# Attention's divided rows turned by SyncE's transposing DMAs as two 16-bit parts, and an output projection on those parts

## The chip, the cores and the metric

The kernel runs on one core of a Trainium2 chip. A core has TensorE (PE; its weight loads are shown as PEld), VectorE (DVE), ScalarE (ACT), GpSimd (POOL) and SyncE (SP), which issues most DMAs. The metric is device time in microseconds (us) of one launch; lower is better.

## The reference

One pre-norm transformer block: attention with a residual, then a mixture of experts with a residual, over 16 sequences of 512 tokens and 256 channels, all float32.

```python
x = L0_attn_x                                    # (16, 512, 256)
x = x + attn(layernorm(x))
x = x + moe(layernorm(x))

def attn(x):                                     # 16 heads of 16 channels
    q, k, v = split(x @ W_attn + b_attn)
    q, k = rope(q), rope(k)                      # angles by head, not by position
    att = softmax(causal(q @ k.T / sqrt(16)))
    y = att @ v                                  # put together to (16, 512, 256)
    return y @ W_proj + b_proj                   # the part that the change is about
```

The mixture (8 experts, the best 2 for each token, and a shared one) is not touched.

## The kernel before

The attention part goes over 16 batches of 512 tokens (`NB`), each in 4 groups of 4 heads (`NG`) and 5 units per group (`UN`): 20 slots per batch, written **g.s** here (slot 2.3 is unit 3 of group 2). Each engine has a `body` that is written out by slot. Tables of slots near the top (`O_T`, `DIVIDE`, `PROJ`, `QK_LOAD` ...) say in which slot an engine does a step; where it stands within the slot is set by the order of the lines of `body`. Engines run their own instructions in order and wait for each other by semaphores.

In every slot TensorE computes a unit's scores into the one pair of banks `pair_s` (`scores`, L1633 and L1653), VectorE takes row maxima from them (`row_max`, L1151 to L1157), and the next slot's scores wait for these. A group's maxima are turned (L1666), made into 16-bit "shift rows" by ScalarE (L885), and brought into row 48 of the tile `q_op` by SyncE (`load_shift`, L448, slot g.2, two DMAs). From the slot g.3 that follows, TensorE computes the scores a second time, transposed and with the shift (`shifted`, L1680; the first one waits for the shift rows), ScalarE takes exponentials (L876), GpSimd cuts off what lies above the diagonal (`select`, L683), and TensorE mixes the values (`mix`, L1706, piece 0 in a slot g.0). `mix`'s output goes to `o_t` (ScalarE, L917).

Beside this, q, k and v of the next batch are made: projections on TensorE (L1571), `qk_rows` on ScalarE, a split in a 16-bit high and low part on GpSimd (`qk_high` L657, `qk_low` L662), stores to DRAM by SyncE (`store_qk`, L426, in slots 2.3 and 0.2) and twelve loads for each half of the heads into `q_op` and `k_op` (`load_qk`, L440, two in each of six slots from the store's slot on; the first waits until the stores have landed).

The batch before is finished meanwhile, in four quarters of 128 tokens (q = 0 to 3) and two halves (j): `o_t` is turned to rows (`transpose_o`, L1722, slots `O_T`), divided by the sums of the softmax (`divide`, L1166 and L1169, slots `DIVIDE`) into `y`, turned again by float32 transposes on TensorE (`transpose_y`, L1730, slots 2.3 and 0.3), copied from PSUM to `y_t` by ScalarE (L934), multiplied with `wp` in float32 (`project_out`, L1741: half 0 in slots 3.3 and 3.4, half 1 whole in slot 1.1), and added to the input and the bias (`residual`, L1180). Then come a layer norm, a split in 16-bit parts and stores to DRAM.

A float32 `matmul` line leaves two records in the trace. After batch 15 two more bodies finish the last batches (the drain). SyncE then reads the stored rows back with transposing DMAs of 512 KB (`logit_columns`, L537), from which TensorE makes the router's logits; behind these the shared expert and the routed experts follow until the end.

The products of 16-bit parts have one helper, which leaves out the product of the two low parts:

```python
for (lh, ll), (rh, rl) in pairs:
    for a, m in ((lh, rh), (lh, rl), (ll, rh)):
        last = nc.tensor.matmul(out, a, m, start=(i == 0), stop=(i == n - 1))
```

## Time and profile before

| | us |
|---|---|
| median of 3 runs | 1665.31 |
| lowest and highest | 1664.85, 1670.92 |
| profiled execution, first to last instruction | 1663.0 |
| batch 8, from its first scores (406.35) to the next batch's (450.23) | 43.88 |
| first scores of batch 0 and of batch 15 | 47.1, 714.9 |
| first matmul of the shared expert | 817.3 |

A row of the time line tells when an instruction began, how long it took, its engine, its line and its tiles (out <- in); in brackets, how long the engine was idle before it and who ended that. The chain of waits goes back from the last instruction of a stretch: at each step to what released it, or to the instruction before it on its engine.

### The profile page before, as it was taken

The page shows a single profiled execution, that of the slowest core. Times are in us where ns is not written, and L with a number is a line of the kernel's source. Part 1 is how long each engine was busy: PE and PEld are TensorE (multiplying, and loading weights), DVE is VectorE, ACT ScalarE, POOL GpSimd, SP SyncE. Part 2 cuts the span into 40 slices and gives each one's busy share as a digit, 9 for nine tenths or more (in the row PEclk, how much of TensorE's full clock was granted, in tenths as well). Part 3 has the DMA queues.
Part 4 walks back from the last instruction along what each step waited for, and adds up shares of the span by engine and source line. Part 5 has one row for each costly group of instructions (what it writes and reads, how often), then busy time and mean ns, then how long its engine had stood idle before and what let it go on. Part 6 is the DMA issues. An engine that isn't in the chain of part 4 may idle for free.

```text
span 1663.0 us, 42374 instructions
## 1 busy us (share of the span) xinstructions
PE 1530.9 (92%) x14774; PEld 1112.8 (67%) x14777; DVE 1053.8 (63%) x1856; ACT 837.1 (50%) x1257; POOL 898.9 (54%) x1123
## 2 busy tenths in 40 slices
PE   3689999999999999977888889999999999999996
PEld 2345555555555555533777778888888888888885
DVE  7568888888888888867377877753333333333332
ACT  1266666666666666655232235534444444444442
POOL 2145555555555555544114667737666666666652
PEclk9699999999999999988699999999999999999999
DMA  2333333333333333353956744346655566556652
GB/s 82 96 90 90 116 116 107 105 112 107 105 113 105 101 110 113 96 124 77 197 162 179 196 113 101 96 110 106 99 103 100 98 102 104 97 99 104 99 81 36
DMA packets 283849, 180.76 MB, mean 109 GB/s; under 512 B 161201, under 2 KB 274353, under 8 KB 283698
## 3 DMA queue, kind: packets, MB, share of 16 engines
q1 hardware_dynamic: 244914, 130.39, 30.4%
q0 software_dynamic: 30208, 35.81, 14.1%
q10 hardware_dynamic: 8576, 12.58, 2.3%
q8 instruction: 91, 1.49, 0.4%
q14 instruction: 60, 0.49, 0.1%
HBM read 84.04 MB, written 60.30 MB: 87 GB/s over the span
## 4 chain that ended last, share of the span: by engine, by line
PE 69%; DVE 10%; DMA 7%; SPq 5%; issue 3%; ACT 3%; POOL 3%; DVEq 0%; POOLq 0%; ACTq 0%
PE bank L1571 20%; PE pair_s L1845 14%; PE bank L1706 7%; PE bank L1845 7%; PE pair_t L1845 7%; PE pair_s L1633 4%; SPq L440 3%; PE pair_t L1680 3%; PE bank L1741 3%; DMA qk_d<-qkl 2%; ACT prob L876 2%; DVE early L1494 1%; PE pair_s L1653 1%; POOL prob L683 1%; PE bank L1722 1%
## 5 line engine op out<-in xcount | busy, mean ns | idle before, releaser
L876 ACT ACTIVATE prob<-pair_t 128x1024 f32<-128x1024 f32 x320 | 327.7, 1024 | 231.0 <-PE pair_t L1680 226.1
L683 POOL TENSOR_SCALAR_AFFINE_SELECT prob<-prob 128x256 f32<-128x256 f32 (+1 forms) x448 | 199.3, 459 | 332.2 <-ACT prob L876 327.7
L803 POOL DMA_INDIRECT out_x<-ysb,tok_rows x136 | 218.8, 1609 | 166.2 <-ACT ysb L1011 115.5
L985 ACT CAST early<-early 128x512 f16<-128x512 f32 (+1 forms) x208 | 125.3, 602 | 336.7 <-DVE early L1494 336.7
L1500 DVE TENSOR_TENSOR early<-early 128x512 f16<-128x512 f32 (+1 forms) x208 | 139.8, 672 | 141.5 <-ACT early L985 141.5
L1494 DVE SCALAR_TENSOR_TENSOR early<-pair_s,h_s,sg 128x512 f32<-128x512 f32 (+1 forms) x104 | 75.9, 730 | 236.9 <-PE pair_s L1845 233.7
L1571 PE MATMUL bank<-wbuf,early 128*128 x1632 | 190.3, 273 | 5.2 <-issue 3.8
L1845 PE MATMUL pair_s<-xt,wbuf 128*128 128x256 f16 (+1 forms) x1728 | 193.9, 267 | 0.1
L765 POOL DMA_INDIRECT tok_d<-tok_w,dest_i x128 | 136.6, 1067 | 104.2 <-DVE dest_i L1420 52.8
L1706 PE MATMUL bank<-prob,v_op 128*32 128x512 f32 (+3 forms) x2048 | 181.0, 448 | 5.2 <-POOL prob L683 5.2
L1151 DVE TENSOR_REDUCE mx<-pair_s 128x2 f32<-128x1024 f32 x128 | 156.8, 1225 | 44.3 <-PE pair_s L1653 42.7
L1845 PEld LDWEIGHTS pair_s<-xt,wbuf 128*128 x1728 | 163.4, 98 | 19.8 <-issue 0.2
L1571 PEld LDWEIGHTS bank<-wbuf,early 128*128 128x128 f16 x1632 | 158.8, 98 | 25.3 <-issue 6.6
L784 POOL DMA_INDIRECT xrow<-xhl_d,tok_rows x136 | 136.3, 1002 | 55.0 <-issue 37.5
L1633 PE MATMUL pair_s<-k_op,q_op 48*128 48x512 f16 (+3 forms) x1024 | 128.7, 310 | 33.9 <-DVE mx L1151 11.5
L1633 PEld LDWEIGHTS pair_s<-k_op,q_op 48*128 48x128 f16 x1024 | 34.8, 94 | 153.7 <-DVE mx L1151 68.7
L1154 DVE TENSOR_REDUCE mx<-pair_s 128x2 f32<-128x768 f32 x128 | 122.0, 953 | 18.9 <-PE pair_s L1653 17.5
L1680 PE MATMUL pair_t<-q_op,k_op 49*128 49x512 f16 (+3 forms) x1024 | 124.7, 301 | 9.9 <-DMA q_op<-m_row 7.8
L977 ACT ACTIVATE sg<-pair_s,silu_s 128x512 f32<-128x512 f32 (+1 forms) x104 | 69.6, 670 | 81.9 <-PE pair_s L1845 68.2
L1845 PE MATMUL bank<-xt,wbuf 128*128 128x256 f16 (+1 forms) x864 | 103.1, 267 | 0.0
L1845 PE MATMUL pair_t<-xt,wbuf 128*128 128x256 f16 (+1 forms) x864 | 102.8, 267 | 0.0
L1845 PE MATMUL pair_s<-xrow,wsh 128*128 128x256 f16 x720 | 86.1, 274 | 16.4 <-DVE early L1494 16.3
(274 smaller groups left out, 2751.0 us busy)
## 6 DMA issues: line engine op xcount, KB each, us to landing
q_op<-qk_d SPq DMA_DIRECT2D x192, 64.0 KB, 2.6
k_op<-qk_d SPq DMA_DIRECT2D x192, 64.0 KB, 2.7
x_in<-in_L_attn_x SPq DMA_DIRECT2D x16, 512.0 KB, 4.1
qk_d<-qkh SPq DMA_DIRECT2D x32, 256.0 KB, 2.2
qk_d<-qkl SPq DMA_DIRECT2D x32, 256.0 KB, 2.6
xres<-in_L_attn_x SPq DMA_DIRECT2D x16, 512.0 KB, 4.7
x_d<-x SPq DMA_DIRECT2D x32, 256.0 KB, 2.2
xhl_d<-xhl SPq DMA_DIRECT2D x32, 256.0 KB, 2.6
```

Of the source, the lines that this page charges most:

```text
L683: last = nc.gpsimd.affine_select(out=v, in_=v, compare_op=ALU.is_ge, fill=0.0, base=0, pattern=[[0, v.shape[1]], [1, P]], channel_multipli ...
L765: pool.indirect_dma_start(out=tok_d, out_offset=bass.IndirectOffsetOnAxis(ap=dest_i[:, t, k:k + 1], axis=0), in_=tok_w[:, t, k, :], in_off ...
L784: pool.indirect_dma_start(out=xrow[:, k % GATHERED], out_offset=None, in_=xhl_d, in_offset=bass.IndirectOffsetOnAxis(ap=tok_rows[:, k, 0:1 ...
L803: pool.indirect_dma_start(out=out, out_offset=bass.IndirectOffsetOnAxis(ap=tok_rows[:, k, 0:1], axis=0), in_=ysb[:, k % ROWS_AHEAD], in_of ...
L876: nc.scalar.activation(prob[:, half, u].rearrange("p a n -> p (a n)"), pair_t[:].rearrange("p a n -> p (a n)"), ACT.Exp, scale=exp_by).the ...
L1151: last = nc.vector.tensor_reduce(dst[:, :, u, 3], pair_s[:], AX_X, ALU.max)
L1500: nc.vector.tensor_tensor(htl2[:, par, 2 * hh:2 * hh + 2, 0:w], hb2[:, hh, 0:2 * w].rearrange("p (c n) -> p c n", c=2), hth2[:, par, 2 * h ...
L1571: last = nc.tensor.matmul(out, a, m, start=(i == 0), stop=(i == n - 1))
L1633: nc.tensor.matmul(ps_s[a][:, lo:lo + P * (q + 1)], q_op[64 * a:64 * a + KR, par, pair, P * q:P * (q + 1)], k_op[64 * a:64 * a + KR, par, ...
L1680: last = nc.tensor.matmul(ps_t[a][:, lo:lo + n], k_op[rows, par, pair, P * k:P * (k + 1)], q_op[rows, par, pair, P * k:], start=start, sto ...
L1706: last = nc.tensor.matmul(ps_o[32 * h:32 * h + 32, P * k:], v_op[:, vpar, k, GH * gg + h, :], pr[:, unit, h % 2, lo:lo + n], start=(piece ...
L1845: last = nc.tensor.matmul(out[:, w * k:w * k + w], stationary, rows[:, x, 0:w], start=(i == 0), stop=(i == 3 * CC - 1))
```

## The change

The tile `y` is now divided and scaled by a power of two in one step. GpSimd splits each quarter into a 16-bit high and low part (`y_split`: a cast and a subtraction into `y_hl`). When a half has both quarters, SyncE turns the 128x1024 16-bit row block by one transposing DMA into `y_t` (`y_columns`). The transposes of `y` on TensorE and ScalarE's copy are gone. `project_out` multiplies 16-bit parts: per 128 tokens six 16-bit matmuls in place of two float32 ones. The scale is taken out in `residual`. Scales and parts of the weights (`wp_h`, `wp_l`, in the tile `cs` that is free by then) are made once, in the prologue; the weights arrive in the tile `y`. The quarters' transposes and divisions move: quarter 2 from slot 3.2 to 3.0, quarter 3 from slots 0.1 and 0.2 to 3.2.

```diff
-        O_T = ((1, 4), (2, 2), (3, 2), (0, 1))
-        DIVIDE = ((2, 1), (2, 2), (3, 2), (0, 2))
-        Y_T, Y_OUT = ((2, 3), (0, 3)), ((3, 1), (0, 4))
+        O_T = ((1, 4), (2, 2), (3, 0), (3, 2))
+        DIVIDE = ((2, 1), (2, 2), (3, 0), (3, 2))
+        Y_SPLIT, Y_COLUMNS = ((2, 2), (2, 3), (3, 1), (3, 3)), ((3, 0), (0, 0))
...
+            def y_columns(bp, j):
+
+                sp.wait_ge(S["yl_done"], 4 * bp + 2 * j + 2)
+                sp.sem_inc(S["sp_passed"], 1)
+                if some(2 * bp + j):
+                    sp.wait_ge(S["pr_in"], 2 * bp + j)
+                    sp.sem_inc(S["sp_passed"], 1)
+                sp.dma_start_transpose(y_t[:], y_hl[:, j].rearrange("p t n -> p (t n)")).then_inc(y_turned[j], 16)
...
                             sp.dma_start(xres[:], xv[b - 1]).then_inc(S["res_in"], 16)
+                        for j, bp in heads_here((g, s), Y_COLUMNS, b, prev, prev2):
+                            y_columns(bp, j)
...
+            def y_split(bp, q):
+
+                k, j = 4 * bp + q, q // 2
+                pool.wait_ge(S["y_done"], k + 1)
+                if q % 2 == 0 and some(bp):
+                    pool.wait_ge(y_turned[j], 16 * bp)
+                high = y_hl[:, j, q % 2, 0:C]
+                nc.gpsimd.tensor_copy(high, y[:, q % 2]).then_inc(S["yh_done"], 1)
+                pool.wait_ge(S["yh_done"], k + 1)
+                nc.gpsimd.tensor_tensor(y_hl[:, j, q % 2, C:], y[:, q % 2], high, ALU.subtract
+                                        ).then_inc(S["yl_done"], 1)
...
-                        for j, bp in heads_here((g, s), Y_OUT, b, prev, prev2):
-                            k = 2 * bp + j
-                            act.wait_ge(S["yT_in"], k + 1)
...
-                            nc.scalar.copy(y_t[:].rearrange("p t c n -> p (t c n)"),
-                                           ps_y[:]).then_inc(S["yT_done"], 1)
...
-                nc.vector.tensor_tensor(y[:, q % 2].rearrange("p (h d) -> p h d", d=HD), ov[:, :, 0:HD],
-                                        rec[:, q % 2].unsqueeze(2).broadcast_to([P, H, HD]),
-                                        ALU.mult).then_inc(S["y_done"], 1)
+                if some(k - 1):
+                    dve.wait_ge(S["yl_done"], k - 1)
...
+                nc.vector.scalar_tensor_tensor(out=y[:, q % 2].rearrange("p (h d) -> p h d", d=HD),
+                                               in0=ov[:, :, 0:HD], scalar=vp_scale[:, 0:1],
+                                               in1=rec[:, q % 2].unsqueeze(2).broadcast_to([P, H, HD]),
+                                               op0=ALU.mult, op1=ALU.mult).then_inc(S["y_done"], 1)
...
-            def transpose_y(bp, j):
-                pe.wait_ge(S["y_done"], 4 * bp + 2 * j + 2)
-                for t in range(2):
-                    for c in range(2):
-                        last = nc.tensor.transpose(ps_y[:, P * (2 * t + c):P * (2 * t + c + 1)],
-                                                   y[:, t, P * c:P * (c + 1)], ident[:])
...
                 if t == 0:
-                    pe.wait_ge(S["yT_done"], 2 * bp + j + 1)
+                    pe.wait_ge(y_turned[j], 16 * bp + 16)
...
-                for c in range(2):
-                    last = nc.tensor.matmul(ps_m[:, 256 * t:256 * t + 256], y_t[:, t, c, :], wp[:, c, :],
-                                            start=(c == 0), stop=(c == 1))
+                last = products(ps_m[:, 256 * t:256 * t + 256],
+                                [((y_t[:, 4 * t + c, :], y_t[:, 4 * t + CC + c, :]), (wp_h[:, c, :], wp_l[:, c, :]))
+                                 for c in range(CC)])
```

Where this puts instructions, first SyncE from the stores of slot 2.3 to the shift rows of slot 3.2 in a middle batch, before (`qk_d` is q and k in DRAM, `m_row` the shift rows; a "waits" names semaphores):

```order
L426 DMA qk_d<-qkl 128x2x512
L440 DMA q_op<-qk_d 16x4x512 [waits qks0,t_in]
L440 DMA k_op<-qk_d 16x4x512
L440 DMA q_op<-qk_d 16x4x512
L440 DMA k_op<-qk_d 16x4x512
L440 DMA q_op<-qk_d 16x4x512
L440 DMA k_op<-qk_d 16x4x512
L440 DMA q_op<-qk_d 16x4x512
L440 DMA k_op<-qk_d 16x4x512
L448 DMA q_op<-m_row 1x8x128 [waits m_done]
```

and the same place now:

```order
L434 DMA qk_d<-qkl 128x2x512
L448 DMA q_op<-qk_d 16x4x512 [waits qks0,t_in]
L448 DMA k_op<-qk_d 16x4x512
L448 DMA q_op<-qk_d 16x4x512
L448 DMA k_op<-qk_d 16x4x512
L448 DMA q_op<-qk_d 16x4x512
L448 DMA k_op<-qk_d 16x4x512
L498 DMA_TRANSPOSE y_t<-y_hl 128x8x128 [waits yl_done,pr_in]
L448 DMA q_op<-qk_d 16x4x512
L448 DMA k_op<-qk_d 16x4x512
L456 DMA q_op<-m_row 1x8x128 [waits m_done]
```

The new DMA stands behind six of the eight loads and ahead of two loads and the shift rows, with two waits of its own.

GpSimd in slots 3.3 to 0.0, before (`prob` is the select's tile, `qkl` the low parts of the next batch's q and k):

```order
L657 CAST qkh<-qkf 128x512 [waits qks1,qkf_done]
L683 AFFINE_SELECT prob<-prob 128x4x128 [waits exp_done]
L683 AFFINE_SELECT prob<-prob 128x2x128 [waits exp_done]
L662 TENSOR_TENSOR qkl<-qkf,qkh 128x512 [waits qkh_done]
L683 AFFINE_SELECT prob<-prob 128x2x128 [waits exp_done] x2
```

and now:

```order
L683 TENSOR_TENSOR y_hl<-y,y_hl 128x256 [waits yh_done]
L717 AFFINE_SELECT prob<-prob 128x4x128 [waits exp_done]
L717 AFFINE_SELECT prob<-prob 128x2x128 [waits exp_done]
L696 TENSOR_TENSOR qkl<-qkf,qkh 128x512 [waits qkh_done]
L681 CAST y_hl<-y 128x256 [waits y_done]
L683 TENSOR_TENSOR y_hl<-y,y_hl 128x256 [waits yh_done]
L717 AFFINE_SELECT prob<-prob 128x2x128 [waits exp_done] x2
L717 AFFINE_SELECT prob<-prob 128x2x128
```

The fourth quarter's split stands between `qk_low` of slot 3.3 and the select of slot 3.4.

TensorE in slot 1.1, from its scores to those of slot 1.2, before (`bank` is a rotating PSUM bank):

```order
L1633 MATMUL pair_s<-k_op,q_op 128x512 [waits max_done]
L1633 MATMUL pair_s<-k_op,q_op 128x512
L1653 MATMUL pair_s<-mask,pick 128x64 x4
L1680 MATMUL pair_t<-q_op,k_op 128x384 [waits exp_done]
L1680 MATMUL pair_t<-q_op,k_op 128x384
L1680 MATMUL pair_t<-q_op,k_op 128x128 x2
L1741 MATMUL bank<-wp,y_t 128x256 [waits m_done,yT_done]
L1741 MATMUL bank<-wp,y_t 128x256 x3
L1633 MATMUL pair_s<-k_op,q_op 128x384 [waits max_done]
```

and now:

```order
L1689 MATMUL pair_s<-k_op,q_op 128x512 [waits max_done]
L1689 MATMUL pair_s<-k_op,q_op 128x512
L1709 MATMUL pair_s<-mask,pick 128x64 x4
L1736 MATMUL pair_t<-q_op,k_op 128x384 [waits exp_done]
L1736 MATMUL pair_t<-q_op,k_op 128x384
L1736 MATMUL pair_t<-q_op,k_op 128x128 x2
L1627 MATMUL bank<-cs,y_t 128x256 [waits m_done,y_cols1]
L1627 MATMUL bank<-cs,y_t 128x256 x11
L1689 MATMUL pair_s<-k_op,q_op 128x384 [waits max_done]
```

The four float32 matmuls (eight records) have become twelve 16-bit ones in the same place, which wait for the DMA's landing in place of ScalarE's copy.

## Rows read from the trace of the kernel before

**Rows 1.** The page, the whole span: busy time, its share and the instructions of each engine.

```profile
PE 1530.9 (92%) x14774; PEld 1112.8 (67%) x14777; DVE 1053.8 (63%) x1856; ACT 837.1 (50%) x1257; POOL 898.9 (54%) x1123
```

**Rows 2.** Stretches: us, busy PE, PEld, DVE, ACT, POOL, clock, DMA share, GB/s.

```profile
406.35:450.23 43.88, 42.72 (x437) 23.30 (x438) 37.92 (x73) 30.20 (x43) 24.37 (x43) 1.00 0.34 104
733.57:743.81 10.24, 8.01 (x53) 2.64 (x53) 3.20 (x4) 4.26 (x6) 3.06 (x6) 0.50 0.67 128
```

**Rows 3.** Time line, TensorE, scores of slot 2.4 (columns as explained above).

```profile
437.21 0.39 PE L1633 MATMUL pair_s<-k_op,q_op 48*128 48x256 f16 x4 [0.20 <-DVE mx L1155]
```

**Rows 4.** Chain of waits, slots 2.2 to 3.3 of batch 8: start, us, what.

```profile
435.48 1.14 POOL qkl L662
...
437.17 2.74 DMA qk_d<-qkl
...
440.07 0.32 SPq L440
...
443.24 0.43 SPq L440
...
443.79 0.64 SPq L448
...
444.47 1.83 DMA q_op<-m_row
...
446.35 0.39 PE pair_t L1680 x2
...
447.31 1.06 PE bank L1741 x4
```

**Rows 5.** Time line, ScalarE, GpSimd and TensorE, slots 3.2 to 0.0 of that batch.

```profile
441.66 0.25 ACT L885 ACTIVATE m_row<-bank 16x128 f16<-16x128 f32 x1
...
448.57 1.15 POOL L662 TENSOR_TENSOR qkl<-qkf,qkh 128x512 f16<-128x512 f32 x1
...
450.26 0.42 POOL L683 TENSOR_SCALAR_AFFINE_SELECT prob<-prob 128x256 f32<-128x256 f32 x1 [0.54 <-ACT prob L876]
...
451.16 1.06 PE L1706 MATMUL bank<-prob,v_op 128*32 128x512 f32 x8
```

**Rows 6.** Line 1680: why TensorE sat idle before it: releaser, us, times.

```profile
  DMA q_op<-m_row: 17.5, 17
```

**Rows 7.** Issues of transposing DMAs, 128 KB (L580), 256 KB (L550): ns least/median/most.

```profile
L580 SPq DMA_TRANSPOSE xt<-xrow x136: 1190/1260/2399, 1092.4 to 1634.8; - x136
...
L550 SPq DMA_TRANSPOSE xrow<-xhl_d x30: 1234/1242/2152, 821.2 to 1067.9; - x30
```

**Rows 8.** Chain of waits, slot 1.1: TensorE's projection of half 1.

```profile
419.32 1.97 PE bank L1741 x8
```

**Rows 9.** Time line, VectorE: the residual behind that projection.

```profile
421.32 0.69 DVE L1180 TENSOR_TENSOR x<-bank,xres 128x512 f32<-128x512 f32 x1 [1.08 <-PE bank L1741]
```

**Rows 10.** Chain of waits in the routed experts: matmuls of 128x256 on 16-bit parts.

```profile
984.12 2.62 PE bank L1571 x24
```

**Rows 11.** Groups by line, GpSimd: count, busy us, mean ns, idle before and releaser.

```profile
L662 POOL TENSOR_TENSOR qkl<-qkf,qkh 128x512 f16<-128x512 f32 x60 | 69.6, 1161 | 0.1
...
L657 POOL CAST qkh<-qkf 128x512 f16<-128x512 f32 x60 | 36.6, 610 | 20.4 <-ACT qkf L846 20.4
```

**Rows 12.** Time line in the drain: SyncE's first 512 KB transpose, TensorE's last logits.

```profile
799.26 2.32 SPq L537 DMA_TRANSPOSE qkl<-xhl_d  x1
...
816.67 0.80 PE L1571 MATMUL bank<-gate_hl,qkl 128*128 128x8 f16 x24 [1.30 <-DMA qkl<-xhl_d]
```

**Rows 13.** Chain of waits, batch 15, SyncE's issues around a 512 KB transpose.

```profile
725.18 2.04 SPq L537
...
728.82 1.59 SPq L440
...
731.48 0.68 SPq L448
```

**Rows 14.** Time line, TensorE, first shifted matmul of batch 15's slot 0.3.

```profile
733.96 0.61 PE L1680 MATMUL pair_t<-q_op,k_op 49*128 49x512 f16 x2 [2.44 <-DMA q_op<-m_row]
```

More of the change, by code:

```diff
@@ L139, in build @@
         wal = sb_a("wal", [P, 2, 3 * C], F32R)
-        wp = sb_a("wp", [P, 2, C], F32)
+        wp_h, wp_l = (cs[:, k].bitcast(F16).rearrange("p (c n) -> p c n", c=2) for k in range(2))
         bcol = sb_a("bcol", [P, 4], F32)
@@ L168, in build @@
         y = sb_a("y", [P, 2, C], F32)
-        y_t = sb_a("y_t", [P, 2, 2, P], F32)
+        y_hl = sb_a("y_hl", [P, 2, 2, 2 * C], F16)
+        y_t = sb_a("y_t", [P, 2 * 2 * CC, P], F16)
+        wp = y
         xres = sb_a("xres", [P, NT, C], F32)
@@ L715, in body @@
                                 input_rstd(b + 2)
+                        for q, bp in heads_here((g, s), Y_SPLIT, b, prev, prev2):
+                            y_split(bp, q)
                         for j, bp in halves_here((g, s), RSTD_B, b, prev, prev2):
@@ L1138, in prologue_qkv, with output_scales @@
                     first_low(i)
+            def output_scales():
+                dve.wait_ge(S["vp_topped"], 1)
+                link.link(dve, nc.vector.tensor_scalar(vp_top[:], vp_top[:], 1e-30, None, ALU.max))
+                link.link(dve, nc.vector.tensor_scalar(vp_top[:].bitcast(I32), vp_top[:].bitcast(I32),
+                                                       0x7F800000, None, ALU.bitwise_and))
+                link.link(dve, nc.vector.reciprocal(vp_inv[:], vp_top[:]))
+                nc.vector.tensor_scalar(vp_scale[:, 0:1], vp_inv[:, 0:1], 16.0, None, ALU.mult)
+                nc.vector.scalar_tensor_tensor(out=out_scale[:], in0=vp_top[:, 0:1], scalar=2.0 ** -18,
+                                               in1=vp_top[:, 1:2], op0=ALU.mult, op1=ALU.mult)
+                nc.vector.tensor_scalar(vp_scale[:, 1:2], vp_inv[:, 1:2], 2.0 ** 14, None, ALU.mult
+                                        ).then_inc(S["vp_done"], 1)
+                dve.wait_ge(S["wph_done"], 1)
+                nc.vector.scalar_tensor_tensor(out=wp_l, in0=wp[:], scalar=vp_scale[:, 1:2], in1=wp_h,
+                                               op0=ALU.mult, op1=ALU.subtract).then_inc(S["wpl_done"], 1)
             prologue()
             prologue_qkv()
+            output_scales()
             def row_max(G, g, u):
@@ L1179, in residual @@
                     dve.wait_ge(x1_stored[j], 16 * bp)
-                nc.vector.tensor_tensor(x1[:, j].rearrange("p t c -> p (t c)"), ps_m[:],
-                                        xres[:, 2 * j:2 * j + 2].rearrange("p t c -> p (t c)"), ALU.add
-                                        ).then_inc(S["x1_done"], 1)
+                nc.vector.scalar_tensor_tensor(out=x1[:, j].rearrange("p t c -> p (t c)"), in0=ps_m[:],
+                                               scalar=out_scale[:],
+                                               in1=xres[:, 2 * j:2 * j + 2].rearrange("p t c -> p (t c)"),
+                                               op0=ALU.mult, op1=ALU.add).then_inc(S["x1_done"], 1)
             def residual_stats(bp, j):
```

34 lines of the change are left out of this document (20 added, 14 removed).

## The prediction

> **What bounds the kernel now.** I read the page first: TensorE is busy for 92% of the span [rows 1]. A busy share does not say what the removal of TensorE work is worth, so I next asked for a table of stretches. One whole batch of the attention part takes 43.88 us with TensorE busy for 42.72, VectorE for 37.92 and GpSimd for 24.37 [rows 2]. TensorE looks like the bound, with VectorE 6 us behind. But the twenty slots of a batch do not add up freely: `scores` of a slot waits for all row maxima of the slot before it, since there is one pair of banks for scores. In slot 2.4, for example, TensorE starts 0.20 us late, released by VectorE's maximum [rows 3]. A slot whose TensorE work is already shorter than scores plus maximum gains nothing by losing more.
>
> So I read the chain of waits over a batch. From slot 2.2 to slot 3.3 it is not TensorE's at all [rows 4]: GpSimd's `qk_low` (435.48, 1.14 us), SyncE's two stores of q and k to DRAM, whose landing takes 2.74 us from 437.17, eight load issues on SyncE from 440.07 to 443.67 (0.43 us each and a gap of 0.04), then the issue of the shift rows at 443.79, its landing 1.83 us after the second of its two issues, and the first shifted matmul at 446.35. The shift rows had been ready since 441.91 [rows 5]: SyncE's queue kept them 1.9 us, and the matmul starts the moment they land. This is not one batch's bad luck. TensorE's first shifted matmul is ended by these rows 17 times, for 17.5 us together [rows 6]. In the other batches the order on SyncE is the same, so I take the slack of this chain as zero to 0.3 us.
>
> **The change, part by part.** Sums are made against the profiled execution, 1663.0 us from first to last instruction; the median of the runs, 1665.3, is 2.3 above it, and I add that at the end. N is 14: batches 1 to 14 have both a previous batch to project and a next one to load.
>
> *SyncE's transposing DMA of half 0 (slot 3.0).* It stands in SyncE's queue behind six of the eight load issues and ahead of the last two and of the shift rows, which are thus held up by all of it. Its data are old by then (GpSimd's second split ends a slot earlier, and SyncE comes to it six issues of 0.47 after 440.07, at 442.9), so its waits cost only their passing: two more gaps and counts, about 0.16 us by the gaps of rows 4. The issue itself: this trace has no DMA of 128 x 1024 between two SBUF tiles. Two rows bracket it [rows 7]: SBUF to SBUF with half the bytes holds SyncE for 1.26 us (least 1.19), and DRAM to SBUF with the same bytes for 1.24. Doubling the bytes between those two added nothing, so I take 1.26; the upper end is twice that, 2.5, if a source in SBUF pays by bytes; the lower end is an ordinary issue, 0.43. Taken: 1.26 + 0.16 = 1.42 us per batch, all of it on the path, N x 1.42 = **+19.9** (ends 8.3 and 37).
> The Trainium skill, page Advanced Engine Details and Errata, section X-Bar Transpose (TRN2), says that transposing DMAs are as fast as regular ones. As to the time for which they hold the queue, the rows disagree: 1.26 against 0.43. By that rule the term would be 14 x (0.43 + 0.16) = 8.3 us.
>
> *What this chain covers.* Between slots 2.2 and 3.3 TensorE now has time to spare, so work moved or removed there is worth nothing: the transposes of `y` that leave slot 2.3, the transposes of `o` that move from slot 3.2 to 3.0 and from 0.1 to 3.2 (0.6 us more in 3.0), the first three splits on GpSimd, and VectorE's divisions in their wider form. Without that cover the added transposes in 3.0 would cost up to 0.6 us a batch. The transposes that leave slot 0.3 free TensorE where it waits for the maximum anyway: zero. ScalarE's copy of `y_t` was off the path: zero.
>
> *The projection of half 1, slot 1.1.* Here the chain runs along TensorE: eight float32 records take 1.97 us [rows 8], and VectorE's residual waits for them, idle 1.08 us [rows 9]. They become twelve 16-bit matmuls of 128x256. Twenty-four such matmuls take 2.62 us elsewhere [rows 10], 0.109 each, so twelve take 1.31: -0.66. VectorE, which carries this stretch right behind TensorE, may return a little with its wider residual; I take -0.56. N x -0.56 = **-7.8** (ends -9.2 and -4).
>
> *The projection of half 0, slot 3.3.* Four records of 1.06 us [rows 4] become six matmuls, 0.65: -0.41. But the fourth split stands on GpSimd right behind `qk_low` of this slot, which ends at 449.72, and ahead of the next select (450.26) that `mix` of slot 0.0 needs at 451.16 [rows 5]. A cast of 128x512 takes 0.61 us and a subtraction 1.16 [rows 11]; half as wide and with two gaps, a split is about 1.0. The select then ends near 451.25 and `mix` starts near 451.3, where with the gain it would have been ready at 450.75. The gain is lost, and 0.14 more. N x 0.14 = **+2.0** (ends -5.7, if splits are cheaper, and +7).
>
> *Half 1's transposing DMA, slot 0.0.* SyncE waits there for the fourth split and may hold up the shift rows of slot 0.2. At slot 0.3 no first shifted matmul of the trace is ended by these rows, so I take zero; if that room is gone, the price is that of half 0.
>
> *The drain.* After the last batch SyncE issues transposing DMAs of 512 KB one behind the other (from 799.26 on, 2.32 us the first) and TensorE's last logits wait for the last of them [rows 12]. Two `y` transposes now stand among these, 1.4 each: +2.8; the second also waits until half 0 is projected. Taken **+3** (ends 1 and 7).
>
> *Prologue.* Maxima and splits of the weights run while VectorE waits for GpSimd and TensorE for the first keys; zero, at most 3 us once.
>
> Sum: 19.9 - 7.8 + 2.0 + 3 = +17.1, so 1680.1 for the profiled execution and **1682** for the median.
>
> **The rivals.** *A: the transposing DMA costs SyncE more than its issue.* The trace has a precedent: in the last batch a transposing DMA of 512 KB (2.04 us) went out among the loads at 725.18, one load issue after it took 1.59 in place of 0.43, and the shift rows followed only at 731.48 [rows 13]. TensorE then stood idle for 2.44 us [rows 14], and its granted clock fell to 0.50, the 1.2 GHz level, for 10.24 us [rows 2]. Half the bytes could add 0.6 us of such stalling per batch (+8), an issue of 2.5 adds 17, and a fallen clock in a few batches 2 to 4 us each (+8). That gives about 1700 to 1715. Against it: the stall I expect is mostly 1 to 1.5 us, shorter than the one before that fall.
>
> *B: the queue is held for no longer than by an ordinary DMA.* Then the first term is 8.3 and the sum 5.5: 1671, no change that can be measured. The skill's rule quoted above would end here; the rows on the time of issue speak against it. A split cheaper than I think, together with an issue at its least, ends here too.
>
> *C: faster.* The shift rows are not held up: the transposing DMA's issue falls into time in which SyncE would have waited. Then only the projections count: -7.8 - 5.7 + 3 = -10.5, or 1655. It decides at a delay of about 0.2 us per batch in place of 1.42. For it: TensorE is the busiest engine and loses work in four slots of each batch. Against it: SyncE issues the eight loads without a break and the shift rows right behind them [rows 4], so there is no waiting time for the DMA to fall into.
>
> **How the numbers follow.** Within 0.5% is about what a measurement of this kernel can tell from no change: 1657 to 1673.6. My forecast, 1674 to 1692, has 0.48; A, up to about 1715, has 0.20; B, 1658 to 1673, has 0.20; C has 0.12. Hence faster 0.12, same 0.20, slower 0.68. The range leaves out C's lower half and A's upper end: 1656 to 1708.
>
> **What would show it.** In the profile after, a transposing DMA on SyncE between the sixth and the seventh load issue, 1.2 to 1.3 us long; the issue of the shift rows 3.3 us after they are ready in place of 1.9; TensorE's first shifted matmul of slot 3.3 idle for 1 to 1.5 us in nearly every batch, where the whole kernel had 17.5 us before; batches of about 45 us in place of 44. Slot 1.1 should be shorter by 0.6 us, `mix` of slot 0.0 should wait for GpSimd's select, and the shared experts should start about 3 us later relative to the last batch. The prediction is wrong if the shift rows go out as soon as before, if the new issue takes 0.5 us or over 2, or if the granted clock falls in slot 3.3.

## The result, and the profile after

The changed kernel takes 1686.97 us (median of 4 runs, 1683.8 to 1687.95), the kernel before 1665.08 beside it: a ratio of 1.0125, interval 1.0105 to 1.0146. It is slower by 1.25%, as forecast; the forecast was 1682, the range 1656 to 1708. The profiled execution spans 1684.8 us, 21.8 more than before.

The page's line of busy times, which answers [rows 1]:

```profile
PE 1501.2 (89%) x14774; PEld 1089.4 (65%) x14777; DVE 1068.9 (63%) x1865; ACT 820.7 (49%) x1226; POOL 957.6 (57%) x1252
```

TensorE is busy for 30 us less and the kernel is 22 us longer. The work did leave TensorE; what was lost is waiting. The rows that answer [rows 4] are the chain of waits in the same place, slots 2.2 to 3.3 of batch 8 (start, us, what):

```profile
445.87 1.17 POOL qkl L696
...
447.60 2.52 DMA qk_d<-qkl
...
450.27 0.32 SPq L448
...
452.51 0.43 SPq L448
...
453.12 1.27 SPq L498
...
454.44 0.58 SPq L448
...
455.61 0.68 SPq L456
...
456.33 1.70 DMA q_op<-m_row
...
458.07 0.41 PE pair_t L1736 x2
```

Six load issues run to 452.94; the transposing DMA (L498) stands there from 453.12 for 1.27 us; the load behind it takes 0.58 us in place of 0.43; the shift rows follow at 455.61. ScalarE had them ready at 452.39, so SyncE's queue kept them 3.2 us, where it had been 1.9 [rows 5]. TensorE's time line in the same batch (start, us, engine, line, operation, tiles; in brackets idle time and its end):

```profile
451.79 0.66 PE L1773 MATMUL bank<-ident,o_t 128*128 128x128 f32 x4
...
458.07 0.39 PE L1736 MATMUL pair_t<-q_op,k_op 49*128 49x512 f16 x2 [0.74 <-DMA q_op<-m_row]
...
458.97 0.83 PE L1627 MATMUL bank<-cs,y_t 128*128 128x256 f16 x6
```

The transposes of quarter 2 now stand in slot 3.0 (0.66 us); the first shifted matmul of slot 3.3 waits 0.74 us for the shift rows although TensorE has more to do on its way there. Over the whole kernel, from the view of waits (engine and line, what it waited for: us in total, times, longest), the kernel before and the changed one:

```profile
PE pair_t L1680 <- DMA q_op<-m_row: 7.8, 7, 2.4
```

```profile
PE pair_t L1736 <- DMA q_op<-m_row: 17.4, 16, 1.9
```

TensorE's first shifted matmul waits for the shift rows 16 times in place of 7, for 17.4 us in place of 7.8. (In [rows 6] the waits of TensorE's weight loads, 10 of 9.7 us, are counted with those of the matmuls; the prediction reads them as 17 waits of one kind.)

To compare runs I cut each of batches 1 to 14 into three stretches, by the starts that the time line gives, and sum each over the 14 batches. **A** goes from the first scores of slot 0.0 to those of slot 2.2, **B** from there to the first shifted matmul of slot 3.3 (SyncE's chain), **C** from that to the next batch's first scores. In us, with the runs of the experiments below:

| kernel | A | B | C | median | ratio to before |
|---|---|---|---|---|---|
| before | 374.1 | 190.9 | 54.2 | 1665.1 | |
| after | 374.2 | 211.7 | 52.9 | 1687.0 | 1.0125 |
| e1_gap | 371.4 | 218.7 | 52.6 | 1696.7 | 1.0202 |
| e2_price | 372.9 | 216.2 | 64.9 | 1703.6 | 1.0244 |
| e3_plain | 376.3 | 202.8 | 50.0 | 1677.5 | 1.0087 |
| e4_late_split | 366.2 | 211.9 | 50.8 | 1679.3 | 1.0094 |
| e5_gaps | 376.2 | 221.4 | 61.0 | 1708.2 | 1.0256 |
| e6_gap_early | 374.8 | 205.3 | 50.0 | 1680.2 | 1.0100 |
| e7_gap_late | 369.4 | 204.9 | 50.0 | 1676.7 | 1.0069 |
| e8_placed | 395.5 | 205.0 | 50.0 | 1699.3 | 1.0210 |
| e9_idle_price | 372.5 | 190.3 | 54.2 | 1663.3 | 0.9991 |
| e10_gap_price | 373.2 | 196.6 | 55.6 | 1670.9 | 1.0033 |
| e11_best_split | 367.5 | 197.4 | 51.6 | 1668.3 | 1.0032 |
| e12_cover | 374.9 | 212.8 | 57.6 | 1694.4 | 1.0180 |

Ratios are against runs of the kernel before beside each (medians 1662.4 to 1665.1); the intervals are given below where they matter, and are 0.13% to 0.33% wide to each side. Two medians of this table that were taken beside different runs of the kernel before can thus differ by up to 2.7 us without a cause in the kernels. The stretches are those of one profiled execution each.

### The profile page after: what moved, and what is told of

It is laid out like the page before. It is cut to its first block, busy times and chain, and to the rows that moved or that the text cites. A ratio compares the mean times of both kernels' runs of the same rounds, so it can differ in the third digit from the quotient of the medians.

```text
span 1684.8 us, 42580 instructions
## 1 busy us (share of the span) xinstructions
PE 1501.2 (89%) x14774; PEld 1089.4 (65%) x14777; DVE 1068.9 (63%) x1865; ACT 820.7 (49%) x1226; POOL 957.6 (57%) x1252
## 3 DMA queue, kind: packets, MB, share of 16 engines
q0 software_dynamic: 30208, 35.81, 13.8%
q8 instruction: 91, 1.49, 0.4%
## 4 chain that ended last, share of the span: by engine, by line
PE 56%; DMA 11%; SPq 10%; DVE 9%; POOL 5%; issue 4%; ACT 4%; ACTq 0%; DVEq 0%; POOLq 0%
PE bank L1627 19%; PE pair_s L1888 13%; PE bank L1888 7%; PE pair_t L1888 7%; SPq L448 6%; PE bank L1762 4%; DMA qk_d<-qkl 4%; ACT prob L914 3%; PE pair_s L1689 3%; POOL qkl L696 2%; DMA k_op<-qk_d 2%; PE pair_t L1736 2%; POOL prob L717 2%; DMA q_op<-m_row 2%; DVE early L1550 1%
## 5 line engine op out<-in xcount | busy, mean ns | idle before, releaser
L717 POOL TENSOR_SCALAR_AFFINE_SELECT prob<-prob 128x256 f32<-128x256 f32 (+1 forms) x448 | 195.5, 450 | 277.0 <-ACT prob L914 261.6
L1627 PEld LDWEIGHTS bank<-wbuf,early 128*128 128x128 f16 x1632 | 158.7, 98 | 24.7 <-issue 6.0
L1736 PE MATMUL pair_t<-q_op,k_op 49*128 49x512 f16 (+3 forms) x1024 | 123.9, 299 | 20.9 <-DMA q_op<-m_row 17.4
```

The source lines that it names most:

```text
L717: last = nc.gpsimd.affine_select(out=v, in_=v, compare_op=ALU.is_ge, fill=0.0, base=0, pattern=[[0, v.shape[1]], [1, P]], channel_multipli ...
L1736: last = nc.tensor.matmul(ps_t[a][:, lo:lo + n], k_op[rows, par, pair, P * k:P * (k + 1)], q_op[rows, par, pair, P * k:], start=start, sto ...
```

## The experiments

The theory: the cost is the time for which the transposing DMA holds SyncE's queue ahead of the shift rows, on a chain without slack. Its rivals: the DMA's traffic slows the loads and the shift rows wherever it stands; or the moved and added work on TensorE and GpSimd costs it.

### e2_price and e9_idle_price: the same DMA, twice, in the kernel before

Only this is added to the kernel before (`turned` is a spare tile, `wah` a part of the weights); in e2_price at slot 3.0 behind the loads, in e9_idle_price at slot 0.2 behind the shift rows:

```diff
+                        if prev and (g, s) == (3, 0):
+                            if some(b - 1):
+                                sp.wait_ge(S["turned_in"], 16 * (b - 1))
+                                sp.sem_inc(S["sp_passed"], 1)
+                            sp.dma_start_transpose(turned[:], wah[:, 0, 0:512].bitcast(F16)
+                                                   ).then_inc(S["turned_in"], 16)
```

> The kernel before, with one addition: in slot 3.0 of each batch SyncE issues a transposing DMA of 128 x 1024 16-bit elements between two tiles that nobody else waits for (it turns a part of the weights into a spare tile), in the place where the changed kernel has its own. Queue theory: the stretch from slot 2.2 to the first shifted matmul grows by 1.27 + 0.15 + a few stretched issues, about 1.5 us in 14 batches: 1665 + 21 = 1686. Engine rival: no engine but SyncE has more to do, so no change, 1665 to 1668. Traffic rival: slower too, but with the load issues behind it stretched, not only pushed back.

> The kernel before with the same added transposing DMA as e2_price, but in slot 0.2 behind the shift rows, where SyncE waits some 2.5 us for the next stores. Queue theory: free, 1663 to 1667. Traffic rival: at least half of what e2_price added (41 us), 1680 or more.

e2_price took 1703.6 us (ratio 1.0244, 1.0213 to 1.0274): 41 us more (37 between the profiled executions) for an instruction for which nobody waits. e9_idle_price took 1663.3 (ratio 0.9991, 0.9977 to 1.0004): nothing. SyncE in e9_idle_price, the shift rows, the added DMA and the next store:

```profile
449.86 1.33 SPq L449 DMA_DIRECT2D q_op<-m_row  x2
451.31 1.27 SPq L499 DMA_TRANSPOSE turned<-wah  x1
453.81 0.37 SPq L427 DMA_DIRECT2D qk_d<-qkh  x1
```

The added DMA's issue is over, and the queue still waits 1.2 us for its next data. So the bytes cost nothing that can be measured in this place, and neither TensorE nor GpSimd has more to do in either kernel. That leaves the traffic in slot 3.0 itself, which e9_idle_price doesn't test. There the rows of e2_price speak against it: in batches without a stretched issue the shift rows go out 5.28 us behind the first load in place of 3.72, and then land in 1.71 us, no later than before (1.72 to 1.92, but for one of 2.75). So the traffic rival falls as the main cause, and the engine rival as a cause of this part: the place in the queue decides. But e2_price is also 17 us dearer than I expected. Stretch B grew by 25 us (21 expected), C by 10.7, which nobody had put there. The first shifted matmul of its batch 7, and what follows (TensorE's time line):

```profile
417.62 0.61 PE L1687 MATMUL pair_t<-q_op,k_op 49*128 49x512 f16 x2 [3.81 <-DMA q_op<-m_row]
...
419.17 2.08 PE L1748 MATMUL bank<-wp,y_t 128*128 128x256 f32 x4
```

and stretch C of that batch and of batch 8 (us, then busy time of PE, PEld, DVE, ACT and POOL with counts, granted clock, DMA share, GB/s):

```profile
417.62:423.87 6.25, 6.25 (x28) 3.04 (x28) 1.23 (x1) 3.45 (x5) 1.74 (x3) 0.54 0.64 193
465.74:469.62 3.88, 3.74 (x29) 2.00 (x30) 1.65 (x3) 3.16 (x5) 1.53 (x2) 1.00 0.76 215
```

After an idle time of 3.81 us the same matmuls run at a granted clock of 0.54 on the mean, near the 1.2 GHz level (0.50), and stretch C takes 6.25 us in place of 3.88; the projection's first four records take 2.08 in place of 1.06 to 1.13. That is the fallen clock of rival A. It came behind six of the 14 waits, of 1.90 to 3.81 us; behind another of 2.72 us (batch 13) the clock stayed at 1.00, so the length of the wait alone doesn't decide. Over the kernel the shifted matmuls waited 32.9 us for the shift rows:

```profile
PE pair_t L1687 <- DMA q_op<-m_row: 32.9, 16, 3.8
```

### e12_cover: does the work in slot 3.0 shield the clock?

The changed kernel loses only 2.8 us to the clock with the same DMA in the same place. It has one thing more there, the transposes moved into slot 3.0. e12_cover is e2_price with them moved too, and with them ScalarE's copy of half 0 (`Y_OUT`):

```diff
-        O_T = ((1, 4), (2, 2), (3, 2), (0, 1))
-        DIVIDE = ((2, 1), (2, 2), (3, 2), (0, 2))
-        Y_T, Y_OUT = ((2, 3), (0, 3)), ((3, 1), (0, 4))
+        O_T = ((1, 4), (2, 2), (3, 0), (3, 2))
+        DIVIDE = ((2, 1), (2, 2), (3, 0), (3, 2))
+        Y_T, Y_OUT = ((2, 3), (0, 3)), ((2, 4), (0, 4))
```

> e2_price (the kernel before with the added transposing DMA in slot 3.0) with the transposes and divisions of the last two quarters moved to slots 3.0 and 3.2, as the changed kernel has them. Theory: SyncE's chain is as long as in e2_price, so slot 3.0's 0.63 us of added work only shorten TensorE's idle time in slot 3.3, and by that the 1.2 GHz stretches behind it (10.7 us in e2_price, 2.8 in the changed kernel) shrink: 1703.6 less 6 to 10, 1694 to 1697. Rival (the work in slot 3.0 adds to the rest): 1703.6 + 14 x 0.63 = 1712. Rival (it is covered and the clock has no part): 1703.

1694.4 us, 9 less than e2_price, within what was expected: B 212.8 against 216.2, C 57.6 against 64.9. The wait for the shift rows:

```profile
PE pair_t L1687 <- DMA q_op<-m_row: 20.6, 16, 2.1
```

It fell by 12.3 us, in batches 1 to 14 by 11.8: 14 x 0.59 = 8.3 is the work that now fills slot 3.0, and the rest is B's 3.4, where issues and landings were stretched less. The work in slot 3.0 was free, for B did not grow by it. And with shorter waits the clock fell in two batches (7 and 11, mean 0.67 and 0.69) in place of six: 2.9 us of stretch C in place of 10.7. (Batch 8's stretch C also took over 4 us, 4.31, but at a clock of 1.00: there TensorE waited for a load.) How much of this is due to the work in slot 3.0, and how much to B's 3.4 us, this one execution doesn't separate. e1_gap and e5_gaps (below) point the same way: with that work the clock fell in 2 of their 14 batches, without it in 11.

### e3_plain: an ordinary DMA in the same place

The `...` stands for the views of the tile and the semaphores. Half 0 of `y` is then not turned, so this kernel computes something else.

```diff
-                sp.dma_start_transpose(y_t[:], y_hl[:, j]...)
+                if j == 0:
+                    sp.dma_start(y_t[:], y_hl[:, j]...)
+                else:
+                    sp.dma_start_transpose(y_t[:], y_hl[:, j]...)
```

> The changed kernel with an ordinary DMA of the same bytes in place of half 0's transposing DMA, in the same place of the queue (so half 0 of y isn't turned, and the projection's values are not the reference's). Queue theory: it holds SyncE for 0.43 us in place of 1.27 (1.49 on the mean with the stretched ones), so 14 x 0.84 to 1.06 = 12 to 15 us go: 1672 to 1675. Rival (any DMA in that place costs the same, by its two waits and its bytes): 1687.

1677.5 us (ratio 1.0087, 1.0060 to 1.0115), 9 us less than the changed kernel (6 by the ratios, 11 between the profiled executions) where I had expected 12 to 15. SyncE, this DMA and the next load:

```profile
448.13 0.54 SPq L499 DMA_DIRECT2D y_t<-y_hl  x1
448.71 0.58 SPq L448 DMA_DIRECT2D q_op<-qk_d  x1
```

It holds the queue for 0.54 us in place of 1.27; the load behind it takes 0.58 us here too. B fell by 8.9 us (0.64 a batch), and the 2.8 us of the clock went too. Not all of the 0.7 us arrives: the shift rows, issued sooner behind the loads, take longer to land (1.95 us on the mean from the second issue in place of 1.81). The Trainium skill, page Advanced Engine Details and Errata, section X-Bar Transpose (TRN2), has transposing DMAs as fast as regular ones; for the landing that is about so here (median 3.4 us against 3.2 from issue to landing), for the queue that issues them it is not.

### e1_gap and e6_gap_early: half 0's DMA where SyncE waits anyway

Behind the two stores of slot 2.3 SyncE waits for their landing. e1_gap puts the DMA there:

```diff
-        Y_SPLIT, Y_COLUMNS = ((2, 2), (2, 3), (3, 1), (3, 3)), ((3, 0), (0, 0))
+        Y_SPLIT, Y_COLUMNS = ((2, 2), (2, 3), (3, 1), (3, 3)), ((2, 3), (0, 0))
...
                             if there and (g, s) == QK_STORE[j]:
                                 store_qk(n, npar, j)
+                            if (g, s) == QK_STORE[j]:
+                                for i, bp in heads_here((g, s), Y_COLUMNS, b, prev, prev2):
+                                    y_columns(bp, i)
```

> The changed kernel, with only half 0's transposing DMA put elsewhere in SyncE's queue: behind the two stores of slot 2.3 and ahead of the first load, where SyncE waits for the stores to land anyway. Queue theory (the cost of the change is the time for which this DMA holds SyncE's queue ahead of the shift rows): the stretch from the start of slot 2.2 to the first shifted matmul falls from 15.12 us to what TensorE's own work needs, 13.52 + 0.34 = 13.86, so 14 x 1.26 = 17.6 us go: about 1669. Traffic rival (it is the added bytes and descriptors that slow the loads and the shift rows, wherever the DMA stands): 1680 or more. Engine rival (the transposes moved to slot 3.0 and the split on GpSimd cost it): no change, 1687.

1696.7 us, 10 more than the changed kernel in place of 18 less. The rows show an oversight of mine, not the traffic: GpSimd's second split, and SyncE's stores, DMA and first load:

```profile
450.64 0.67 POOL L687 TENSOR_TENSOR y_hl<-y,y_hl 128x256 f16<-128x256 f32 x1
```

```profile
448.63 1.19 SPq L434 DMA_DIRECT2D qk_d<-qkl  x1
451.48 1.27 SPq L498 DMA_TRANSPOSE y_t<-y_hl  x1
452.94 0.44 SPq L448 DMA_DIRECT2D q_op<-qk_d  x1
```

The split ended at 451.31. SyncE, whose queue is in order, stood at the DMA's wait from 449.82 on, and all eight loads with it; the first went out 3.1 us behind the stores (3.8 in most other batches), where 1.9 to 2.2 are usual. In e6_gap_early the split moves to slot 2.2, right behind the first:

```diff
-        Y_SPLIT, Y_COLUMNS = ((2, 2), (2, 3), (3, 1), (3, 3)), ((2, 3), (0, 0))
+        Y_SPLIT, Y_COLUMNS = ((2, 2), (2, 2), (3, 1), (3, 3)), ((2, 3), (0, 0))
```

> The kernel of e1_gap, in which the transposing DMA waited for GpSimd's second split (ended 451.3) when the stores had gone out at 449.8, with this split moved to slot 2.2, right behind the first. The DMA can then go out at once and be over before the stores have landed. Queue theory (only the time for which the queue is held beyond its own waiting counts): landing as in the changed kernel (2.1 us), loads 3.6 in place of 5.47, the stretch from slot 2.2 to the first shifted matmul at TensorE's own 13.86 in place of 15.12, and no fall of the clock in slot 3.3: 14 x 1.26 + 2.8 = 20 us less than the changed kernel, about 1667. Traffic rival (the DMA's own bytes make the stores land late, wherever it is issued): landing stays near 3.7 and the time near e1_gap's 1693.

1680.2 us (ratio 1.0100, 1.0073 to 1.0127): 17 less than e1_gap, but 13 more than expected. The same rows:

```profile
443.19 0.68 POOL L687 TENSOR_TENSOR y_hl<-y,y_hl 128x256 f16<-128x256 f32 x1
```

```profile
442.24 0.93 SPq L434 DMA_DIRECT2D qk_d<-qkl  x1
444.03 1.27 SPq L498 DMA_TRANSPOSE y_t<-y_hl  x1
445.49 0.45 SPq L448 DMA_DIRECT2D q_op<-qk_d  x1
```

The split ends 0.7 us behind the second store, so the DMA is over at 445.30 and the first load goes out 2.3 us after the stores where 1.9 to 2.2 are usual, in most other batches 2.8. The rest is in the loads (4.13 us from first to last on the mean, 3.68 before, some stretched to 1.3 to 1.9 us, see below) and in the landing of the shift rows (2.12 us on the mean in place of 1.89).

### e10_gap_price: the same gap, with data that are always ready

e2_price's addition at slot 2.3, between stores and loads (the diff above with `(2, 3)`).

> The kernel before with the added transposing DMA of e2_price behind the two stores of slot 2.3 and ahead of the first load, with data that are always ready. What was left of the cost in e6_gap_early (14.67 us from slot 2.2 to the first shifted matmul where TensorE alone needs 13.86) came from its waiting for GpSimd's split, or from the DMA's presence next to the stores and loads. Queue theory: SyncE issues it within the 2.1 us in which it waits for the stores, so it is free: 1664 to 1667, chain 13.6 to 13.8. Rival (next to the stores it makes them land later and the loads slower): chain 14.3 or more, 14 x 0.7 = 10 us and more, 1674 or more.

1670.9 us (ratio 1.0033, 1.0017 to 1.0050), between the two. In quiet batches (without stretched issues) B is 13.4 us against 13.2 before, so the gap is nearly free, but not wholly: the stores land 2.17 to 2.22 us behind the end of their issue in eight batches, where 2.01 to 2.03 were usual before. Six of the 14 batches have 14.4 to 15.6, where before three had over 14, and behind one of them the clock fell (C 55.6). There, issues and landings are stretched (last section); whether the DMA's presence makes that likelier isn't settled by this run.

### e4_late_split, e7_gap_late, e11_best_split: GpSimd's splits

```diff
-        Y_SPLIT, ... = ((2, 2), (2, 3), (3, 1), (3, 3)), ...
+        Y_SPLIT, ... = ((2, 2), (2, 3), (3, 1), (3, 4)), ...   (e4_late_split)
+        Y_SPLIT, ... = ((2, 2), (2, 2), (3, 1), (3, 4)), ...   (e7_gap_late, with e6's place)
+        Y_SPLIT, ... = ((2, 1), (2, 2), (3, 1), (3, 4)), ...   (e11_best_split, with e6's place)
```

> The changed kernel with GpSimd's fourth split one slot later, behind the select of slot 3.4 in place of ahead of it. Theory: mix of slot 0.0 gets its select in time, and slot 0.0 loses the 0.31 us that it gained in 13 batches: 4 us, about 1683; SyncE then waits longer for the split in slot 0.0, and its shift rows go out some 1.3 us later there, within the 1.5 us that they have. Rival (they don't have that room): slot 0.3 grows by up to 1 us, 14 us in all, 1697. Rival (the 0.31 us of slot 0.0 come from elsewhere): 1687.

1679.3 us (ratio 1.0094, 1.0071 to 1.0117), nearly 8 less than the changed kernel (5 by the ratios, 8.4 between the profiled executions). The mix of slot 0.0 no longer waits for a select, and the split runs beside it:

```profile
457.23 0.40 POOL L681 CAST y_hl<-y 128x256 f16<-128x256 f32 x1
...
457.70 1.06 PE L1762 MATMUL bank<-prob,v_op 128*32 128x512 f32 x8
457.71 0.68 POOL L683 TENSOR_TENSOR y_hl<-y,y_hl 128x256 f16<-128x256 f32 x1
```

Slot 0.0 lost 0.32 us in the mean of batches 3 to 13, 5 us in all; another 2.8 us come from slot 1.4, where fewer landings were slow (last section), which I take for chance. The shift rows of slot 0.2 had the room: slot 0.3 is unchanged at 1.90.

> e6_gap_early and the fourth split behind the select of slot 3.4 as in e4_late_split, together. If the two costs stand apart from each other: e6_gap_early less 5 to 7 us, about 1660 to 1662. If the later split only moves a wait to SyncE in slot 0.0 once the rest is gone: as e6_gap_early.

1676.7 us: 3.4 less than e6_gap_early where 5 to 7 were expected. A fell by 5.4 and the profiled execution by 5.0, so the two costs stand apart.

> e7_gap_late with half 0's splits a slot earlier each, the first in slot 2.1 (where GpSimd waits 0.9 us for the exponentials) and the second right behind qk_low in slot 2.2, so that half 0's DMA can go out as soon as the stores are out. Queue theory: the landing of the stores falls from 2.64 to 2.1, qk_low comes 0.2 later: 14 x 0.3 to 0.5 = 4 to 7 us less than e7_gap_late, 1670 to 1673. If the DMA's presence is what costs there: no less than e7_gap_late, 1677.

1668.3 us (ratio 1.0032, 1.0014 to 1.0049), 8.5 less than e7_gap_late. B is 197.4 us, 14.1 a batch where TensorE alone needs 13.8, and the wait for the shift rows is below that of the kernel before:

```profile
PE pair_t L1740 <- DMA q_op<-m_row: 6.7, 7, 2.6
```

Up to the last batch's last scores this kernel is 3.3 us ahead of the kernel before (756.7 against 760.0); it loses 6.3 in the drain (63.6 against 57.3), where its `y` transposes stand among SyncE's 512 KB ones. So most of what SyncE's queue had cost came back: of the 20.8 us that the change put on stretch B this kernel has 6.5 left, about what the transposes moved into slot 3.0 cost once no wait covers them (14 x 0.6 = 8.4, an estimate from slot 3.0's growth). The projection's gain doesn't show in the end. Why the drain is 4.3 us longer than the changed kernel's isn't shown.

### e5_gaps and e8_placed: both halves moved

e5_gaps puts half 1's DMA behind the stores of slot 0.2 (with e1_gap's place for half 0) and the transposes of quarters 2 and 3 back to slots 3.2 and 0.1; e8_placed has half 0 as in e6_gap_early, half 1's behind the shift rows of slot 0.2, its last split in slot 0.1.

```diff
+        O_T, DIVIDE = ((1, 4), (2, 2), (3, 2), (0, 1)), ((2, 1), (2, 2), (3, 2), (0, 2))    (e5_gaps)
+        Y_SPLIT, Y_COLUMNS = ((2, 2), (2, 3), (3, 2), (0, 2)), ((2, 3), (0, 2))             (e5_gaps)
+        O_T, DIVIDE = ((1, 4), (2, 2), (3, 2), (0, 1)), ((2, 1), (2, 2), (3, 2), (0, 1))    (e8_placed)
+        Y_SPLIT, Y_COLUMNS = ((2, 2), (2, 2), (3, 2), (0, 1)), ((2, 3), (0, 2))             (e8_placed)
```

> The changed kernel with both transposing DMAs where SyncE waits for stores to land (half 0 behind the stores of slot 2.3, half 1 behind those of slot 0.2), and the transposes and divisions of the last two quarters back in the slots that they had before (3.2 and 0.1, 0.2), their splits in slots 3.2 and 0.2. Queue theory: the chain from slot 2.2 to the first shifted matmul is as in the kernel before, slots 3.0 and 0.0 lose the 0.63 and 0.31 us that the change gave them, and only the shorter projections are left: 14 x (0.30 + 0.50) = 11 us less than before, some 4 us of which the loads of half 1 take back in slot 1.4, and 1 to 3 us more in the drain: 1656 to 1662. Traffic rival: the added DMAs slow the loads and the shift rows there too, 1668 or more.

> All that the theory says: half 0's transposing DMA behind the stores of slot 2.3 with both its splits in slot 2.2; half 1's behind the shift rows of slot 0.2 and ahead of the stores there, where SyncE has 2.5 us to wait; transposes and divisions of the last two quarters in slots 3.2 and 0.1, which had room before. Queue theory: chain from 2.2 to 3.3 as in the kernel before, 13.6, slot 3.3 shorter by 0.30 and slot 1.1 by 0.50 in 14 batches, 11 us less than before, of which the loads of half 1 take back up to 4 and the drain 2: 1657 to 1660, faster than the kernel before by 0.3% to 0.5%. Rival (there is no place in which these DMAs are free): 1668 or more.

1708.2 and 1699.3 us: both far off. e5_gaps repeats e1_gap's oversight in both places, and without the work in slot 3.0 its waits brought the clock down (C 61.0). In e8_placed it is stretch A, 395.5. GpSimd's `qk_low` and the split behind it, and SyncE's DMA and store in slot 0.2:

```profile
424.52 1.17 POOL L703 TENSOR_TENSOR qkl<-qkf,qkh 128x512 f16<-128x512 f32 x1
...
426.11 0.67 POOL L690 TENSOR_TENSOR y_hl<-y,y_hl 128x256 f16<-128x256 f32 x1
```

```profile
426.95 1.28 SPq L498 DMA_TRANSPOSE y_t<-y_hl  x1
428.42 0.98 SPq L434 DMA_DIRECT2D qk_d<-qkh  x1
```

`qk_low`'s data were ready for the store at 425.7; the DMA ahead of it waited for the split until 426.8, and the store went out at 428.42. Slots 1.3 and 1.4 grew by 0.93 and 0.94 us against the kernel before (mean of batches 3 to 13), waiting for the shift rows and loads that stand behind it; slot 0.2 grew by 0.56, which I did not follow up. The same DMA with old data was free in this very place (e9_idle_price).

## Why the prediction was right, point by point

The mechanism was the forecast one: a transposing DMA in front of the shift rows holds a queue that has no slack, and costs more than the shorter projections give. That the sum came within 5 us is partly luck, since several terms were off by 3 to 5 us and offset each other. Terms for batches 1 to 14, predicted and measured on the two traces (us):

| term | predicted | measured |
|---|---|---|
| SyncE's DMA of half 0 (stretch B) | +19.9 | +20.8 |
| projection of half 0, slot 3.3 (stretch C) | -5.7 | -4.2 |
| clock in stretch C | 0 (rival A: +8) | +2.8 |
| split ahead of the select, slot 0.0 | +7.7 | +2.8 |
| projection of half 1, slot 1.1 | -7.8 | -6.4 |
| loads of half 1, slot 1.4 | 0 | +3.9 |
| other slots of A | 0 | -0.2 |
| prologue, batches 0 and 15, drain | +3 | +2.2 |
| sum | +17.1 | +21.7 |

**SyncE's queue.** Right in place and cause; the size is near by luck. The new issue takes 1.27 to 1.28 us in 10 of the 14 batches, and 1.42 to 2.50 in four (1.49 on the mean; I had taken 1.26); its waits add 0.18 and the load behind it 0.15. On the mean the shift rows go out 5.59 us behind the first load in place of 3.82, which is 1.77 later and not 1.42: 24.7 us in the 14 batches. Only 20.8 arrived, for two reasons that the sum didn't have. The stores and the shift rows landed about 0.1 us sooner each, and in seven batches of the kernel before the rows had landed 0.04 to 0.20 us before TensorE wanted them (the prediction had read 17 waits where there were 7, but its slack of zero to 0.3 us was right). Half 1's DMA in slot 0.0 was taken as free and was: slot 0.3, which could have waited behind it, takes 26.5 us in the 14 batches in both kernels. e9_idle_price and e2_price show the cause: the same instruction is free where the queue waits and costs 25 us of stretch B where it does not. Rival B (an ordinary hold) and C (not held up) fell with the 1.27.

**The cover.** Slot 3.0 grew by 0.63 us a batch and the wait in slot 3.3 absorbed it: e12_cover, with the same work, has no longer a stretch B than e2_price without it. What I had not seen is that the cover also pays: it shortens the waits behind which the clock can fall (e12_cover).

**Slot 1.1.** The twelve matmuls take 1.47 us, not 1.31, since these came out at 0.123 us each and not at 0.109 [rows 10]. The chain of waits, and VectorE's residual behind it, which answer [rows 8, 9]:

```profile
430.24 1.47 PE L1627 MATMUL bank<-cs,y_t 128*128 128x256 f16 x12
...
431.74 0.75 DVE L1235 SCALAR_TENSOR_TENSOR x<-bank,out_scale,xres 128x512 f32<-128x512 f32 x1 [0.58 <-PE bank L1627]
```

The slot gained 0.50 in place of 0.56. Half 0's projection gained 0.30 in place of 0.41 for the same reason.

**Slot 0.0.** The step was right: the split stands between `qk_low` and the select, and mix waits. GpSimd's split and select, and TensorE's mix:

```profile
461.24 0.40 POOL L681 CAST y_hl<-y 128x256 f16<-128x256 f32 x1
...
461.71 0.67 POOL L683 TENSOR_TENSOR y_hl<-y,y_hl 128x256 f16<-128x256 f32 x1
...
462.33 0.41 POOL L717 TENSOR_SCALAR_AFFINE_SELECT prob<-prob 128x256 f32<-128x256 f32 x1
...
462.89 1.06 PE L1762 MATMUL bank<-prob,v_op 128*32 128x512 f32 x8 [0.32 <-POOL prob L717]
```

I had put the loss at 0.55 a batch; mix starts 0.31 us later in its slot, in 11 of the 14 batches. The split itself takes 1.14 us, more than my 1.0; the select had had some slack that I hadn't counted. With half 0's gain mis-sized too, the two errors nearly cancel: predicted +2.0, measured -1.4.

**Rival A** came in a small part: in batches 3 and 5 the new issue was stretched to 2.50 and 2.29 us, the matmul's wait was 1.93 and 1.71 us, and the clock fell behind it. By the prediction's own signs of being wrong (an issue over 2 us, a fallen clock in slot 3.3) these two batches go against it, and the forecast had put the clock at nothing. The wait of batch 3, stretch C of batch 3 and, for comparison, of batch 8 (columns as above), and half 0's first projection matmuls in batch 3:

```profile
229.38 0.45 PE L1736 MATMUL pair_t<-q_op,k_op 49*128 49x512 f16 x2 [1.93 <-DMA q_op<-m_row]
```

```profile
229.38:234.41 5.03, 4.66 (x33) 2.12 (x34) 1.62 (x3) 3.15 (x5) 2.54 (x4) 0.66 0.78 233
458.07:461.65 3.58, 3.14 (x33) 1.67 (x34) 2.81 (x5) 3.07 (x5) 1.87 (x3) 1.00 0.58 176
```

```profile
230.78 1.46 PE L1627 MATMUL bank<-cs,y_t 128*128 128x256 f16 x6
```

Six matmuls take 1.46 us there, 0.83 in batch 8. In the other batches, with waits of 0.69 to 1.63 us, the clock stayed at 1.00. Seven of the 14 waits are near 0.7 us, so the sign of 1 to 1.5 us in nearly every batch did not come either.

**What the prediction missed** is slot 1.4: nothing of it was in the sum, and it gave 3.9 us back. The scores of slot 2.0 need the last load of half 1. In batch 10 TensorE waits for it, and the chain of waits leads from there back to a slow landing of the stores of slot 0.2:

```profile
530.93 0.39 PE L1689 MATMUL pair_s<-k_op,q_op 48*128 48x512 f16 x2 [1.32 <-DMA k_op<-qk_d]
```

```profile
513.86 4.10 DMA qk_d<-qkl
...
525.47 5.41 DMA k_op<-qk_d
```

Such landings (3.5 to 3.7 us behind the second store's issue, 1.8 to 2.2 otherwise) are in 6 of the 14 batches, 3 of 14 before. A slow landing lengthens slot 1.4 by 0.82 us on the mean now and by 0.37 before: the shorter slot 1.1 took away half a microsecond of slack that had hidden part of them, so part of what was saved there was given back one chain further on. With three slow landings that would be about 1.4 us (3 x 0.45, an estimate); the rest of the 3.9 comes from there being six, and e4_late_split and e11_best_split, with the same slot 1.1, have three and two.

**The drain** cost 2.0 us from the last scores of batch 15 to the shared expert (59.3 against 57.3), near the 3 predicted. The two DMAs among the 512 KB transposes:

```profile
812.36 1.23 SPq L498 DMA_TRANSPOSE y_t<-y_hl  x1
...
821.03 1.29 SPq L498 DMA_TRANSPOSE y_t<-y_hl  x1
```

## What to carry to other kernels

An instruction's price in an in-order DMA queue is what stands behind it: the same transposing DMA cost 41 us in one slot and nothing in another. Before moving it into a waiting place, see when its own data are ready, for a wait at the head of the queue holds everything behind it (e1_gap, e8_placed). And where TensorE waits, work put ahead of the wait can be worth more than nothing, since a clock that falls behind a wait slows what comes after: over the 14 traces it did so behind 25 of the 40 waits of 1.7 to 3.8 us ahead of slot 3.3's shifted matmul in batches 1 to 14. Conversely, a slot made shorter only gains up to the slack of the next chain.

## What the runs showed of the hardware

The stretched issues on SyncE are not random. Between the first scores of batch 1 and of batch 15, 17 of SyncE's 609 DMA issues in the changed kernel took over 0.35 us longer than the median of their line; for all 17 a packet of the queues that the page calls "instruction" began during the issue or up to 1.2 us ahead of it, which holds for only 118 of all 609. In the kernel before it is 20 of 20 (107 of all 582), and over the traces of all 14 kernels 306 of 306, where 1588 of all 8447 issues have such a packet. The longest transposing DMA, in batch 3, and that queue's line in the stretch from 223 to 226 us (packets, MB, share):

```profile
223.21 2.50 SPq L498 DMA_TRANSPOSE y_t<-y_hl  x1
```

```profile
q8 instruction: 1, 0.02, 3.0%
```

The slow landings have the same mark. All six of the changed kernel in slot 0.2, and all three of the kernel before, have such a packet start 1.7 to 2.2 us behind the first store's issue, and the landings of 1.8 to 2.2 us have none there. In batch 10, from 515 to 518 us, in which the stores' own traffic all but ended at 516 (26 small packets, 0.02 MB, from then on) and the landing came at 517.96:

```profile
q8 instruction: 1, 0.02, 2.2%
```

That is a coincidence in time over 9 landings and 306 issues, not an experiment: no run here moved these packets on purpose. It suggests, without showing it, that a microsecond here or there in single batches, in any of these kernels, hangs on where such packets fall, and that some of the 3 to 4 us of slot 1.4 may come and go with any edit.
